# A graph attention layer on one core: edge inputs and stored rows move for three chunks and for two at a time

## Reference

```python
xl = jnp.einsum('ni,nio->no', x, hetero_w[node_type]) + hetero_b[node_type]
src, dst = (edge_index[0], edge_index[1])
ete = _lrelu(edge_type_emb[edge_type])
eae = _lrelu(edge_attr @ edge_attr_w)
x_i = xl[dst]
x_j = xl[src]
alpha = _lrelu(jnp.concatenate([x_i, x_j, ete, eae], axis=-1) @ att_w)
amax = jax.ops.segment_max(alpha, dst, num_segments=N)
alpha = jnp.exp(alpha - amax[dst])
denom = jax.ops.segment_sum(alpha, dst, num_segments=N)
alpha = alpha / (denom[dst] + 1e-16)
msg = jnp.concatenate([x_j, eae], axis=-1) @ lin_w * alpha
out = jax.ops.segment_sum(msg, dst, num_segments=N)
```

## Time and profile before

| what | value |
|---|---|
| median of 3 runs | 5827.29 us |
| lowest and highest run | 5796.54 and 5832.6 us |
| profiled execution, its own time | 5821.55 us |
| profiled execution, span from first to last instruction | 5819.7 us |
| mean granted TensorE clock, as a share of full speed | 0.762 |
| share of the span busy: PE, DVE, POOL, ACT | 59%, 44%, 48%, 15% |

### The profile page before, as it was taken

How to read it: one execution, slowest core, us unless ns; L and a number is a source line. 1 busy time by engine, 2 the same in 40 slices (tenths; PEclk the granted TensorE clock), 3 DMA queues, 4 the chain that set the end, 5 groups by cost and what they waited for, 6 DMA issues and landing times.

```text
span 5819.7 us, 64841 instructions
## 1 busy us (share of the span) xinstructions
PE 3413.9 (59%) x21563; PEld 1921.9 (33%) x21563; DVE 2540.0 (44%) x6672; ACT 878.1 (15%) x2080; POOL 2783.2 (48%) x2793
## 2 busy tenths in 40 slices
PE   3456565665665565555666565666665666665660
PEld 2233333333333333333333333333333333333340
DVE  6343443443443444344444444444444444443464
ACT  2011111111111111111111111111111111111120
POOL 2554454454454444444554445455454454444417
PEclk7677777777787787777777777787777777777785
DMA  6111121121121121111211211211211211211112
GB/s 187 26 44 42 42 54 43 42 53 42 42 53 42 42 50 44 42 42 42 54 42 46 48 42 43 51 44 42 53 42 42 53 42 42 53 42 42 47 36 72
DMA packets 187871, 284.25 MB, mean 49 GB/s; under 512 B 74956, under 2 KB 142782, under 8 KB 186752
## 3 DMA queue, kind: packets, MB, share of 16 engines
q1 hardware_dynamic: 72864, 159.20, 9.5%
q0 software_dynamic: 90368, 55.56, 7.7%
q10 hardware_dynamic: 24288, 64.79, 3.1%
HBM read 207.03 MB, written 72.29 MB: 48 GB/s over the span
## 4 chain that ended last, share of the span: by engine, by line
another core or an unknown queue 37%; PE 29%; issue 17%; DVE 15%; POOL 2%; DMA 1%; DVEq 0%; SPq 0%; ACT 0%; POOLq 0%; ACTq 0%
PE ps_misc L678 21%; PE ps_pick L690 6%; DVE dst_f L1021 3%; DVE dscore L1055 2%; DVE sums L1148 2%; DVE gath L1048 1%; DVE node_buf L1083 1%; DVE h L1042 1%; POOL hib L515 1%; DVE onehot L1068 1%; PE ps_msg L722 1%; PE ps_attr L699 0%; DVE node_buf L1102 0%; PE ps_misc L645 0%
## 5 line engine op out<-in xcount | busy, mean ns | idle before, releaser
L481 POOL DMA_INDIRECT gath<-table_dram,meta x2675 | 2672.8, 999 | 2877.0 <-DMA meta<-meta_in 2003.3
L678 PE MATMUL ps_misc<-parts,dst_f 128*128 128x462 bf16 x9450 | 2345.3, 405 | 694.4 <-issue 615.4
L678 PEld LDWEIGHTS ps_misc<-parts,dst_f 128*128 128x128 bf16 x9450 | 988.7, 107 | 1921.5 <-issue 1187.0
L690 PE MATMUL ps_pick<-s_dst,onehot 122*128 122x128 bf16 x9375 | 736.5, 232 | 1402.7 <-DVE dscore L1055 895.8
L1055 DVE TENSOR_REDUCE dscore<-ps_pick 128x4 f32<-128x512 f32 x875 | 538.0, 629 | 1660.9 <-remote 1462.5
L690 PEld LDWEIGHTS ps_pick<-s_dst,onehot 122*128 122x128 bf16 x9375 | 609.2, 104 | 1559.0 <-DVE dscore L1055 948.5
L1042 DVE TENSOR_TENSOR h<-ps_misc,sel_mask 128x462 f32<-128x462 f32 x450 | 285.7, 635 | 1384.2 <-remote 1020.6
L575 ACT ACTIVATE wts<-args 128x50 f32<-128x50 f32 x125 | 30.7, 246 | 3484.4 <-DVE args L1126 2719.8
L588 ACT COPY rows<-sums 128x825 f32<-128x825 f32 x125 | 223.5, 1788 | 1080.6 <-DVE sums L1148 1080.6
L1021 DVE TENSOR_SCALAR dst_f<-dst_f,part_group 128x128 bf16<-128x128 f16 x1750 | 355.7, 284 | 0.9 <-DMA dst_f<-sel_code_dram 0.9
L1048 DVE TENSOR_REDUCE gath<-h 128x33 f32<-128x462 f32 x450 | 281.3, 625 | 2.7
(11 more groups left out here) (230 smaller groups left out, 1215.1 us busy)
## 6 DMA issues: line engine op xcount, KB each, us to landing
hib<-digit_dram SPq DMA_DIRECT2D x125, 612.5 KB
rows_dram<-rows ACTq DMA_DIRECT2D x125, 437.5 KB
gath<-table_dram,meta POOLq DMA_INDIRECT x2675
attr<-edge_attr_t_in SPq DMA_DIRECT2D x125, 200.0 KB
dst_f<-sel_code_dram SPq DMA_DIRECT2D x125, 128.0 KB
hib<-digit_dram SPq DMA_DIRECT2D x250, 50.0 KB
rows_dram<-gath ACTq DMA_DIRECT2D x1, 8575.0 KB, 46.8
hib<-digit_dram SPq DMA_DIRECT2D x250, 25.0 KB
```

The costliest lines, as they stand in the source:

```text
L481: nc.gpsimd.indirect_dma_start(gath[u][:, t, :], None, table_dram, bass.IndirectOffsetOnAxis(ap=meta_sb[u][:, t:t + 1], axis=0)).then_inc( ...
L678: last = nc.tensor.matmul(ps_sel[:, j % 2, 0:VW * GN], sel_onehot[:, g, j * P:(j + 1) * P], parts[:, k, g, :], start=(g == 0 and k == 0), ...
L690: last = nc.tensor.matmul(ps_pick[:, g % 2, j * LO:(j + 1) * LO], onehot[0:KD, t * P:(t + 1) * P], s_dst[0:KD, k, :], start=(k == 0), stop ...
```

## The change

The buffers of the five chunks become parts of one tensor each (`meta_all`, `attr_all`, `hib_all`, `rows_all`; the codes were already side by side in `dst_f`). Two groups are formed, chunks 0 to 2 and chunks 3 and 4. SP waits for the sum of a group's last chunk and then issues one set of eight transfers for the whole group, each three or two times as long. ACT stores the rows of a group once, after its last chunk. All waits on `meta_in`, `attr_in`, `hib_in`, `code_in` and `stored` go by the group. What is computed, and the order of the work on PE, DVE and POOL, stays.

```diff
+GROUPS = ((0, 3), (3, 5))
+GROUP_OF = (0, 0, 0, 1, 1)
...
+            def load_hib(c, k):
+                u0, u1 = GROUPS[k]
+                for d, (n, at) in enumerate(zip(DIGITS, DIGIT_AT)):
+                    sp.dma_start(hib_all[at:at + n, u0:u1, :].rearrange("p a e -> p (a e)"),
+                                 digit_dram[d, ds(c + u0, u1 - u0), :].rearrange("a e -> (a e)")
+                                 .partition_broadcast(n)).then_inc(hib_in[k], 16)
...
+            def load_meta(c, k):
+                u0, u1 = GROUPS[k]
+                sp.dma_start(meta_all[:, u0:u1, :], meta[:, ds(c + u0, u1 - u0), :]).then_inc(meta_in[k], 16)
...
             with sp.Fori(1, ITERS) as i:
-                for u in range(U):
-                    sp.wait_ge(sums_ready, count(i * U + u + 1 - U))
-                    sp.dma_start(meta_sb[u][:], meta[:, ds(i * U + u, 1), :].rearrange("p a m -> p (a m)")).then_inc(
-                        meta_in[u], 16)
-                    load_hib(i * U + u, u)
-                    load_code(i * U + u, u)
-                    load_attr(i * U + u, u)
...
+                for k, (u0, u1) in enumerate(GROUPS):
+                    sp.wait_ge(sums_ready, count(i * U + u1 - U))
+                    load_meta(i * U, k)
+                    load_hib(i * U, k)
+                    load_code(i * U, k)
+                    load_attr(i * U, k)
...
                 for u in range(U):
-                    pool.wait_ge(meta_in[u], (i + 1) * 16)
+                    pool.wait_ge(meta_in[GROUP_OF[u]], (i + 1) * 16)
...
-                act.wait_ge(rows_sums, count(c + 1))
-                act.dma_start(rows_pm[:, ds(c * T, T), :], rows[u][:]).then_inc(stored[u], 16)
+                for k, (u0, u1) in enumerate(GROUPS):
+                    if u == u1 - 1:
+                        act.wait_ge(rows_sums, count(c + 1))
+                        act.dma_start(rows_pm[:, ds((i * U + u0) * T, (u1 - u0) * T), :].rearrange("p e f -> p (e f)"),
+                                      rows_all[:, u0:u1, :].rearrange("p a m -> p (a m)")).then_inc(stored[k], 16)
...
-                dve.wait_ge(code_in[u], (i + 1) * 16)
+                dve.wait_ge(code_in[GROUP_OF[u]], (i + 1) * 16)
```

More of the change, by code:

```diff
@@ L144, in gnn_kernel @@
         dst_i = hi_f[:].bitcast(i32)
-        meta_sb = [sb(f"meta{u}", [P, META], i32) for u in range(U)]
-        attr_sb = [sb(f"attr{u}", [G * F_EDGE, TG * P]) for u in range(U)]
-        hib_sb = [sb(f"hib{u}", [P, T * P], bf16) for u in range(U)]
+        meta_all = sb("meta_all", [P, U, META], i32)
+        attr_all = sb("attr_all", [G * F_EDGE, U, TG * P])
+        hib_all = sb("hib_all", [P, U, T * P], bf16)
+        rows_all = sb("rows_all", [P, U, T * RW])
+        meta_sb = [meta_all[:, u, :] for u in range(U)]
+        attr_sb = [attr_all[:, u, :] for u in range(U)]
+        hib_sb = [hib_all[:, u, :] for u in range(U)]
         gath = [sb(f"gath{u}", [P, T, YW]) for u in range(U)]
-        rows = [sb(f"rows{u}", [P, T, RW]) for u in range(U)]
+        rows = [rows_all[:, u, :].rearrange("p (t f) -> p t f", f=RW) for u in range(U)]
         onehot = sb("onehot", [P, T * P], bf16)
@@ L173, in gnn_kernel @@
         sel_node = sb("sel_node", [P, SEL])
-        code_sb = [dst_f[:, (NG + u) * (TSM * P // 2):(NG + u + 1) * (TSM * P // 2)].bitcast(mybir.dt.float16)
-                   for u in range(U)]
+        code_all = dst_f[:, NG * TSM * P // 2:(NG + U) * TSM * P // 2].bitcast(mybir.dt.float16)
+        code_sb = [code_all[:, u * TSM * P:(u + 1) * TSM * P] for u in range(U)]
         sel_onehot = dst_f[:, 0:NG * TSM * P // 2].bitcast(bf16).rearrange("p (g e) -> p g e", g=NG)
@@ L277, in gnn_kernel @@
         codes_out = sem("codes_out")
-        code_in = [sem(f"code_in{u}") for u in range(U)]
+        code_in = [sem(f"code_in{k}") for k in range(len(GROUPS))]
         sel_first_ready = sem("sel_first_ready")
@@ L286, in gnn_kernel @@
         gather_turns = sem("gather_turns")
[L287 to L289 removed]
+        meta_in = [sem(f"meta_in{k}") for k in range(len(GROUPS))]
+        attr_in = [sem(f"attr_in{k}") for k in range(len(GROUPS))]
+        hib_in = [sem(f"hib_in{k}") for k in range(len(GROUPS))]
         gathered = [sem(f"gathered{u}") for u in range(U)]
[L291 removed]
+        stored = [sem(f"stored{k}") for k in range(len(GROUPS))]
         attr_mm = sem("attr_mm")
@@ L387, in _ @@
             sp.dma_start(dst_i, dst_tmajor).then_inc(dst_in, 16)
-            for u in range(U):
-                sp.dma_start(meta_sb[u][:], meta[:, u, :]).then_inc(meta_in[u], 16)
+            for k in range(len(GROUPS)):
+                load_meta(0, k)
             sp.wait_ge(zeroed, 2)
@@ L397, in _ @@
                              att_w[2 * F_IN + F_EDGE:2 * F_IN + 2 * F_EDGE, :]).then_inc(diag_in, 16)
-            for u in range(U):
-                load_attr(u, u)
+            for k in range(len(GROUPS)):
+                load_attr(0, k)
             sp.wait_ge(tab_sb, NODE_ITERS + 2)
@@ L414, in _ @@
             sp.wait_ge(digits_out, 16 * len(DIGITS))
-            for u in range(U):
-                load_hib(u, u)
+            for k in range(len(GROUPS)):
+                load_hib(0, k)
             sp.wait_ge(codes_ready, 1)
@@ L483, in _ @@
                             bass.IndirectOffsetOnAxis(ap=meta_sb[u][:, t:t + 1], axis=0)).then_inc(gathered[u], 16)
-            for u in range(U):
-                pool.wait_ge(stored[u], 16 * ITERS + 1)
+            for k in range(len(GROUPS)):
+                pool.wait_ge(stored[k], 16 * ITERS + 1)
             flag = is_unsorted(pool)
@@ L695, in attr_product @@
             def attr_product(i, u):
[L697 removed]
+                pe.wait_ge(attr_in[GROUP_OF[u]], (i + 1) * 16)
                 for b in range(2):
```

35 lines of the change are left out of this document (16 added, 19 removed).

## The result

The changed kernel takes **6435.8 us** (median of 4 runs, 6411.7 to 6439.2), the kernel before 5820.0 beside it (5796.5 to 5832.6): ratio **1.105**, 95% interval 1.101 to 1.110, slower. 6240 was predicted, with a range up to 6420: the right sign, but 196 us too little, and 16 us outside the range.

The account below looks back on a forecast made before the run. PE nearly stopping while POOL issues gathers was taken as the bound. Per iteration, 136.8 us gathers + 88.4 pause work + 12.6 restarts = 237.8, 17.5 above 220.3; over 24 iterations +420, so 6240 us, range 5790 to 6420.

Parts of the forecast that it names:

- PE nearly stops in runs of gathers: While POOL issues gathers, PE was said to fall to 0.36 matmuls a us, against 7.18 without gathers.
- Because of the longer runs, and not the rest of the change: Five gather stretches an iteration becoming two was the large term, +17.5 us an iteration, +420 us; other parts taken as nothing.
- The gather time: Time per iteration in which POOL issues gathers: 136.8 us, in two runs of 81.8 and 55.0 us.
- the restart: PE starting late and at a low clock after each gather run: 6.3 us each, 12.6 for two an iteration.
- the matmuls under gathers: PE's matmuls during an iteration's two gather runs: 117 and 107, together 224 instead of 484.
- the wait for codes, taken as 0: DVE's new chunk 3 wait for next-iteration codes: 8 to 9 us, hidden in the long gather run; uncovered, +216 us.
- Clock: TensorE's mean granted clock over the program should change little, with longer stretches at either level.
- Tied to PE's program: Rival: PE stops at places of its own program, not from gathers; no change, 5822 (0.14), or bare codes wait, 6040 (0.14).
- Under gathers by time: Faster rival: PE's work under gathers follows their time, not their runs; 473 matmuls there, 203.2 us an iteration, 5411 us, chance 0.08.
- The loads' issue on the path: Faster rival: load issue and set-up bound the loop; three sets fewer of 3.0 us save 216 us, 5606 us, chance 0.04.
- Theory B: Follow-up experiments' rival explanation: the later codes and larger loads cost the time; bare codes wait some 15 us an iteration, 360 us.

Follow-up runs that it names:

- cut runs: Changed kernel with GpSimd idling for two fills of an unused tile before every seventh gather of a chunk: 5182 us beside 5730, ratio 0.904.
- the short runs: Changed kernel with POOL waiting, before a chunk's gathers, for the scan three chunks back, loads still grouped: 5615.7 us beside 5730.4, ratio 0.980.
- the index lists alone: Kernel before with only the meta loads grouped, three at chunk 2 and two at chunk 4: 6384 us beside 5867, ratio 1.088.
- the codes come early: Changed kernel with the select codes loaded right behind the index lists, ahead of the digits: 6316.7 us beside 5730.4, ratio 1.102.
- the stopping chip: Kind of chip, or condition of one, on which the unchanged kernel before took 5820, 5867 and 5730 us in three comparisons.
- the quick chip: Kind of chip, or condition of one, on which the unchanged kernel before took 4079, 4088 and 4089 us in three comparisons.
- fixed pauses: Fills before every seventh gather: changed kernel with two 0.904, three 1.415, one 1.131; kernel before with two 1.270, each against the kernel before.

## Why the prediction was right, and where it fell short

*PE nearly stops in runs of gathers*: right for the chip of the comparison, and now shown by removal (fewer gathers 3387, cut runs 5182, and plain reads 3314 within the limit named there). *Because of the longer runs, and not the rest of the change*: right, 516 of 551 us; the short runs gave it all back.

*The sum.* The gather time was near (135.1 us for 136.8). Two terms failed, by about the same amount. **The first is the restart**: 6.3 us for each of two pauses, 12.6 together. By the same sum the changed kernel loses 111.5 - 672 / 7.18 = 17.9 us an iteration, 11.8 behind the long run and 6.1 behind the short one. In the iteration shown it is 112.8 - 666 / 7.18 = 20.0, with 12.4 and 7.7; with the index lists alone 107.1 - 88.3 = 18.8. The 6.3 itself was taken from two different things, the pauses of an average iteration and the matmuls of one. With the average of both, the kernel before loses (83.5 - 401 / 7.18) / 5 = 5.5 a pause. The two slow beginnings shown cost 14.7 - 27 / 7.18 = 10.9 and 11.8 - 15 / 7.18 = 9.7; the longer pause gets some of it back later, at 7.6 matmuls a us. On average the 40th matmul of a pause starts 11.3 us after the last gather in the kernel before, and 14.6 to 14.9 us after it in the changed one. So a restart after a run of 54 to 81 us is later than one after 28 us, for which I had taken them over. Why was not tried, and the first matmuls of the pauses are not of the same kinds.

**The second is the matmuls under gathers**, 224 predicted and 180 found (215 without the late codes). They hang on *the wait for codes, taken as 0*. It was 15.2 us long for 8 to 9, and it kept PE waiting in the first quarter of the long run: the start that I said would not be lost by coming late was in part lost, 87 matmuls there and not 117. I had put 3.5 MB at 272 to 311 GB/s; what moved was 4.96 MB at 236, since I had left out `attr`, the smaller pieces of digits and the gathers. The price was small beside a bare wait of 24 x 15.2 = 365 us: 35 us net between the two kernels of one comparison, and between 0 and 102 when the codes come early. Together: 237.8 - 1.7 of gathers + 5.2 for 37 more matmuls in pauses + 5.3 of restarts = 246.6, where the scans give 245.9.

A small slip beside these: the windows of the earlier trace rows count an instruction that lies across an edge in both, so that 859 is some 10 too many; 18 selected tiles of 21 matmuls, 375 picks, and 95 others make 848 an iteration.

*Clock*: "should change little" was wrong; 0.762 to 0.727. Both runs of gathers have a mean of 0.60 to 0.61, where the five runs of the earlier trace rows have 0.68 to 0.88.

*The rivals.* Tied to PE's program: falls, no place in the program stops with plain reads or with 95% of the gathers left out. Under gathers by time: would have needed 351 matmuls, there were 180. The loads' issue on the path, 5606: not in the changed kernel, where SP waits 5708 us; the most that grouping was seen to bring is the paced kernel's 2% on the stopping chip and 0.1 to 0.2% on the quick one. The rule on coalescing small transfers in the Trainium skill's "DMA: Bandwidth & Descriptors", section "Rules for kernel authors", thus has little to act on here. What I had no case for is the quick chip: 1.000 there for the grouped index lists. The Trainium skill's "SBUF — State Buffer", section "Who interferes with whom", which the prediction weighed, is borne out by the quick chip (490 matmuls in 64 us beside gathers) and contradicted by the stopping one (24).

*Open.* What in the gathers stops PE, and why in one condition and not in the other. One thing in the trace goes beyond the prediction's reading of the earlier trace rows: not only does PE start little, what it has finished is also seen late. The 84 selection matmuls, four tiles, are recorded as over by 181.6 us, but DVE took up the last two tiles 25 and 75 us after their last matmul. The kernel before first, then the last tile with plain reads on the stopping chip, where it was 0.1 us:

```profile
202.46 0.64 DVE L1042 TENSOR_TENSOR h<-ps_misc,sel_mask 128x462 f32<-128x462 f32 x1 [27.58 <-remote]
257.06 0.64 DVE L1042 TENSOR_TENSOR h<-ps_misc,sel_mask 128x462 f32<-128x462 f32 x1 [53.29 <-remote]
```

```profile
179.86 0.64 DVE L1041 TENSOR_TENSOR h<-ps_misc,sel_mask 128x462 f32<-128x462 f32 x1 [2.79 <-PE ps_misc L677]
```

Waits of DVE that end in "remote", a release that the profile ties to no instruction of the core, come to 1462.5 + 1020.6 = 2483 us in the kernel before and 161.2 + 9.4 = 171 with two fills, and there are none in any trace of the quick chip, nor with plain reads. In the crawl of the earlier trace rows most picks stand 2.80 us apart and last 0.27 us. Whether PE gets its instructions late, its signals leave late, or both have one cause, no run parts; the ends of matmuls in a trace are modelled, but their starts lie before 181.6 us too. Theory B's other half, larger loads, is excluded as a cause of the loss, not as a small gain.

## What to carry to other kernels

Where an engine crawls beside another's long burst, count its work inside bursts and in gaps, and treat an edit that merges bursts as a loss until shown otherwise, even when it only batches loads: here the index list's arrival was what had cut the gathers into runs. Keep such pacing explicit, by a wait on the consumer's progress: against the kernel before the paced kernel took 0.980 on the stopping chip and 0.998 to 0.999, next to nothing, on the quick one, while fixed pauses won 10% on one and lost 13 to 42% on the other. Repeat a surprising bottleneck in another comparison before building on it, price a restart after the length of stop that it will follow, and take the time and the work of such a sum from the same iterations.

## What the runs showed of the hardware

- The same kernel took 5730 to 5867 us in three comparisons and 4079 to 4089 in three others; one of either kind ran on a chip with the number 6. Beside indexed gathers TensorE started 24 matmuls in 64 us in the first (granted clock 0.52) and 490 in the second (1.00); with 95% of the gathers left out the two took 2927.5 and 2932.1 us from the first scan to the last.
- A plain read of the same size (128 rows of the same table), from the same queue, had TensorE start 470 matmuls in those 64 us where it had started 24 beside indexed ones, with the reads in shorter runs. It also held GpSimd for less, on average 0.60 us against 1.00 for a gather on the stopping chip and 1.12 on the quick one; the quick chip's part 5:

```profile
L481 POOL DMA_DIRECT2D gath<-table_dram x2675 | 1579.3, 599 | 1463.5 <-DMA meta<-meta_in 1357.8
```

- Six pauses of GpSimd of some 2.9 us each in 64 us brought 418 matmuls back.
- Beside indexed gathers on the stopping chip, VectorE took up finished results of TensorE as late as 75 us after their last matmul; with plain reads there, the same four tiles were taken up within 0.1 us.
